# Three projection and post-processing steps moved by one place in the step table of one attention layer

## The chip, the cores and the metric

The kernel runs on one core of a Trainium2 chip. The metric is the device time of one launch in microseconds (us), the median of three executions. A profiled execution gives the trace from which all rows below come. The core has a matrix engine (PE, its weight loads are shown as PEld), a vector engine (DVE), a scalar engine (ACT), a general engine (POOL) and a queue engine (SP) that here only issues DMAs. POOL issues small DMAs too. The engines run on their own and meet at semaphores.

## What is computed

Four transformer blocks follow each other on x of 4 batches x 256 tokens x 256 channels, with one context of the same shape. The first has two cross-attentions with 16 heads of 128 channels and an MLP; the second one cross-attention with 16 heads of 16 channels and an MLP; the third is the one that the change touches; the fourth is a grouped-query attention and a layer norm. Cut to what matters, the third is:

```python
h = jnp.concatenate([x, latents], axis=1)          # 256 context rows, then 256 token rows: 512 keys
q = (latents @ q_w + q_b).reshape(b, k_len, 16, 16)
kv = (h @ kv_w + kv_b).reshape(b, p + k_len, 16, 16, 2)
attn = jnp.einsum('bkhd,bnhd->bhkn', q, kmat) / 16
attn = jnp.where(full_mask, attn, -jnp.inf)        # the mask covers the context keys
attn = jax.nn.softmax(attn, axis=-1)
attn_out = einsum('bhkn,bnhd->bkhd', attn, v) @ out_w + out_b + residual
out = rmsnorm(attn_out, postnorm_w)
out = jax.nn.gelu(out @ mlp_w1 + mlp_b1) @ mlp_w2 + mlp_b2
return out + residual
```

Here `x` is the context and `latents` are the 256 tokens that the block before left.

## The kernel before

One program is written out for all five engines by hand. Every operation stands in an engine's stream in the order in which Python emits it, and waits with `wait_ge` on semaphores that count what others have done. Numbers that PE multiplies are split into a high and a low part; a projection is three matmuls (lines 125 to 127: high by high, high by low, low by high) for each half of the channels.

The layers after the first block are made by the `heads_*` functions (lines 1934 to 2311), layer 2 being the one of the change. It works in steps. A step handles two units (a unit is 128 queries of one head against all 512 keys), so a batch of 16 heads is 16 steps (`TB`), four batches are 64 steps, and 7 more drain the pipeline. Below, "step n" is the n-th of these, and "place k" is n modulo 16 inside a block of 16. In step n

- PE multiplies queries by keys for the two units of step n (line 1983, 512 columns each, three PSUM banks in turn), then keys by queries for the two units of step n-5 (line 2001, four matmuls of 256 columns, two banks), then at places 1, 5, 9 and 13 the weighted sums of four heads (line 2069), then the table's post and preparation work of this step, then filler matmuls on constant tiles (line 2113) where the step has neither sums nor a projection: two, or one if the step has post work (`fill_step`). At even steps it ends with the transpose of the row maxima of the two steps before (line 2079).
- DVE takes the row maxima of the two units (line 2236): the first, then the table's work, then the second.
- ACT copies the transposed maxima to `rows` (line 2173), does its part of the table's work, then the exponentials of the two units of step n-5 (line 2159).
- POOL splits the maxima into two parts (lines 2274 and 2276), for the transpose, and sends the finished rows by two small DMAs into the query tile Q (line 2290), where the matmuls of line 2001 read them at the third step after the transpose.

What else is done when is set by two tables. `IN_LAYER[2]` prepares the next batch (b = 1, 2, 3, in blocks 0, 1, 2): `q0 q1` and `k0 k1` project queries and context keys on PE into one bank, `x0 x1` the token keys into another, `v0 v1` and `v2 v3` the values; `qh`, `kh`, `xh` are the high parts on ACT (line 1602, one step later), `ql`, `kl`, `xl` the low parts on DVE (line 1641, one step later); `maskrow` is made on POOL (line 1708, two steps later). `q_out`, `k_out`, `x_out` and `mask_out` are DMAs of SP that spread these parts over the partitions of the tiles Q and K of the next batch: six DMAs for each of q, k and x (line 1468) and two for the mask (line 1491). SP has no steps: it takes its list in order and waits at each entry for what that needs. `POSTS[2]` finishes the batch before, in blocks 1, 2 and 3 (table place k is step 16b+6+k, so 4 is place 10): `po0` and `po1` are four transposes each on PE of the summed heads (line 1738), `on0` and `on1` are a reciprocal and a product on DVE one step later (lines 1772 and 1774). `po1` uses the bank that `on0` reads, and waits for it:

```python
w.wait_ge(S["h_on"], s.po(b, q))                    # L1736
for g in range(4):
    z = pe.transpose(s.MB[:, g * 128:g * 128 + 128], ...)
```

At step 48, so behind the last of these DMAs, SP's list has four weight loads of 256 KB (`piece_sp`, line 277), which wait until the parts that stood in the same staging tile have been sent (`spread_done`). A batch's first step waits (`ready`, line 1964) until its Q and K are complete.

Of the kernel before, what the change touches and what calls it, by code (L numbers as in the profile page):

```python
# [1123 lines left out]
def attn_end(c, w):  # L1124
# [49 lines left out]

# [2 lines left out]
HELD = {1: ("kvtq", "tkqv"), 2: ("kvtqxw", "tqkvw"), 3: ("kvtq", "tqkv")}  # L1177

POSTS = {1: {2: ["po0", "on0"], 3: ["po1", "on1"], 4: ["onT", "oth"], 5: ["otl"], 6: ["c0"], 7: ["c1", "y"]},
# [3 lines left out]

# [1309 lines left out]
```

## Time and profile before

| | |
|---|---|
| Median of three executions | 1269.28 us (1266.02, 1269.28, 1271.29) |
| The profiled execution | 1269.28 us, of which the trace spans 1267.8 us |
| PE / PEld busy | 1223.9 us (97%) / 1033.9 us (82%) |
| DVE / ACT / POOL busy | 891.0 us (70%) / 783.1 us (62%) / 600.0 us (47%) |
| Mean granted PE clock | 0.994 of full speed |
| Layer 2's steps 0 to 63 | from 860.7 to about 1001 us |

Busy time is what the instructions take from start to end. Matmuls overlap, so a busy PE can still be one that waits a little at each instruction; the start of one instruction to the start of the next tells more than its duration. Rows of the timeline merge equal instructions that follow each other; in brackets stands how long the engine had been idle and what ended it. The granted clock is 1.0 at 2.4 GHz and 0.5 at 1.2 GHz.

### The profile page before, as it was taken

Reading aid. Unit: us, or ns where it says so; the run is one execution under the profiler, and the core shown is the slowest. Engines: PE = TensorE matmul, PEld = TensorE weight load, DVE = VectorE, ACT = ScalarE, POOL = GpSimd, SP = SyncE. Lnnn points to the kernel's source line nnn. Section 1 sums busy time; section 2 is a strip of 40 time slices with the busy share of each in tenths; the row PEclk is TensorE's granted clock in tenths of the full one; section 3 lists DMA queues with packets and bytes.
Section 4 is the critical chain, followed back from the end, with each engine's and each line's share of the span. In section 5 each row is a group of like instructions: output and inputs, shape, how many; then the busy total and the mean of one; then the engine's idle time right before and its main releaser. Section 6 shows DMA issues by size and latency. Waiting matters only on the chain. (4 is left out here: it accounts for less than half of the span.)

```text
span 1267.8 us, 27226 instructions
## 1 busy us (share of the span) xinstructions
PE 1223.9 (97%) x9982; PEld 1033.9 (82%) x9982; DVE 891.0 (70%) x2304; ACT 783.1 (62%) x1889; POOL 600.0 (47%) x966
## 2 busy tenths in 40 slices
PE   8999999999999999999989999899999889999997
PEld 7999999999999999999978565786665578666664
DVE  5887867779877777878855776536677664667764
ACT  4876666668866666667864655756665653555553
POOL 3884555558865554556841533504443331334333
PEclk9999999999999999999999999999998999999999
DMA  5441001104420100101411220122212012121100
GB/s 170 152 139 32 29 26 32 33 27 133 134 85 26 34 26 26 34 26 58 123 34 51 80 79 3 51 77 85 73 59 64 2 57 74 53 69 37 45 11 18
DMA packets 56820, 75.03 MB, mean 59 GB/s; under 512 B 11312, under 2 KB 30576, under 8 KB 56688
## 3 DMA queue, kind: packets, MB, share of 16 engines
q1 hardware_dynamic: 51568, 72.75, 18.7%
q8 instruction: 79, 1.29, 0.4%
q0 software_dynamic: 5120, 0.56, 0.3%
q14 instruction: 53, 0.43, 0.1%
HBM read 49.46 MB, written 1.05 MB: 40 GB/s over the span
## 5 line engine op out<-in xcount | busy, mean ns | idle before, releaser
L1095 POOL TENSOR_SCALAR E<-E,rl 128x256 f32<-128x256 f32 x256 | 243.6, 962 | 210.1 <-DVE rl L980 210.1
L2159 ACT ACTIVATE PT<-bank 128x512 f32<-128x512 f32 x320 | 176.5, 593 | 112.4 <-PE bank L2012 56.0
L846 ACT ACTIVATE QTh<-bank,bqs 128x256 fp32r<-128x256 f32 x128 | 60.8, 475 | 156.1 <-PE bank L127 155.9
L2242 DVE CUSTOM_DVE_ANT_0 Em<-bank,M 128x256 bf16<-128x256 f32 x256 | 95.1, 420 | 53.8 <-PE bank L1987 22.3
L856 ACT ACTIVATE E<-bank,nm 128x257 f32<-128x257 f32 x256 | 119.5, 481 | 1.2 <-DVE nm L950 1.1
L984 DVE TENSOR_TENSOR PTl<-bank,PTh 128x512 fp32r<-128x512 f32 x128 | 88.0, 687 | 27.3 <-ACT PTh L868 26.8
L2236 DVE TENSOR_REDUCE nm<-bank 128x1 f32<-128x512 f32 x128 | 83.6, 684 | 33.1 <-PE bank L1983 30.5
L2001 PE MATMUL bank<-Q,K 51*128 51x256 f32 (+1 forms) x640 | 104.1, 323 | 2.8 <-DMA Q<-rows 0.9
L957 DVE SCALAR_TENSOR_TENSOR QTl<-bank,bqs,QTh 128x256 fp32r<-128x256 f32 x128 | 61.5, 481 | 64.0 <-ACT KT L847 63.2
L868 ACT CAST PTh<-bank 128x512 fp32r<-128x512 f32 x128 | 75.2, 588 | 43.1 <-PE bank L771 43.1
L2290 POOL DMA_DIRECT2D Q<-rows x96 | 54.4, 568 | 95.5 <-ACT rows L2173 95.5
L950 DVE TENSOR_REDUCE nm<-bank 128x1 f32<-128x257 f32 x256 | 95.4, 414 | 3.4 <-PE bank L127 3.4
L2069 PE MATMUL bank<-PT,V 128*32 128x256 f32 x1280 | 87.4, 392 | 2.6 <-ACT PT L2159 2.6
L125 PE MATMUL bank<-KT,QTh 128*128 128x258 f32 x256 | 83.3, 326 | 3.4 <-issue 3.2
L2001 PEld LDWEIGHTS bank<-Q,K 51*128 51x128 f32 (+1 forms) x640 | 67.6, 187 | 20.4 <-ACT PT L2159 10.1
L771 PE MATMUL bank<-ident,E 128*128 128x128 f32 x512 | 76.7, 272 | 0.0
L990 DVE SCALAR_TENSOR_TENSOR OTl<-bank,cols,OTh 128x256 fp32r<-128x256 f32 x128 | 60.7, 474 | 18.2 <-ACT OTh L874 18.2
L126 PE MATMUL bank<-KT,QTh 128*128 128x258 f32 x256 | 73.3, 286 | 0.0
L2285 POOL DMA_DIRECT2D Q<-rows x64 | 37.7, 591 | 74.1 <-ACT rows L2173 71.2
L127 PE MATMUL bank<-KT,QTl 128*128 128x258 f32 x256 | 72.3, 282 | 0.0
L125 PE MATMUL bank<-PTh,Vh 128*128 128x256 f32 x256 | 71.8, 281 | 0.0
L127 PE MATMUL bank<-PTh,Vl 128*128 128x256 f32 x256 | 71.7, 280 | 0.0
(438 smaller groups left out, 4423.2 us busy)
## 6 DMA issues: line engine op xcount, KB each, us to landing
stage<-in_wts SPq DMA_DIRECT2D x99, 256.0 KB, 3.3
U<-in_vrows SPq DMA_DIRECT2D x64, 256.0 KB, 2.7
K<-stage SPq DMA_DIRECT2D x48, 128.0 KB
Q<-stage SPq DMA_DIRECT2D x48, 128.0 KB
K<-stage SPq DMA_DIRECT2D x48, 64.0 KB
Q<-stage SPq DMA_DIRECT2D x48, 64.0 KB
K<-xh SPq DMA_DIRECT2D x16, 128.0 KB, 2.9
Q<-rows POOLq DMA_DIRECT2D x96, 4.0 KB, 1.8
```

The source lines that it names most:

```text
L125: pe.matmul(o, wh, xh, start=first, stop=False, skip_group_check=skip)
L127: return pe.matmul(o, wl, xh, start=False, stop=last, skip_group_check=skip)
L771: m = pe.transpose(s.PTB[:, k * 256 + t * 128:k * 256 + t * 128 + 128], s.E[:, i % 3, t, k * 128:k * 128 + 128], c.ident[:])
L856: m = act.activation(s.E[:, i % 3, t, 0:257], bank[:, 0:257], ACT.Exp, bias=s.nm[:, r, t:t + 1], accum_out=s.ls[:, r, t:t + 1])
L950: dve.tensor_reduce(s.nm[:, r, t:t + 1], bank[:, 0:257], AX.X, ALU.max, negate=True).then_inc(S["dve_max"])
L984: dve.tensor_tensor(s.PTl[:], s.PTB[:].rearrange("p (a b) -> p a b", a=2), f32(s.PTh[:]), ALU.subtract).then_inc(S["dve_pt"])
L1095: m = pool.tensor_scalar(s.E[:, i % 3, t, 0:256], s.E[:, i % 3, t, 0:256], s.rl[:, r, t:t + 1], None, ALU.mult)
L2001: z = pe.matmul(s.STB[y][:, 256 * e:256 * e + 256], s.K[r][at, q // s.rp, o:o + 128], s.Q[r][at, q // s.blocks, :], start=l != 3 or e == 0 ...
L2069: z = pe.matmul(s.OB[32 * q:32 * q + 32, 0:256], s.V[b % s.NV][:, k, (4 * g + q) // s.rep, :], s.PT[(i0 + q) % s.NPT][:, k, :], start=k == ...
L2159: act.activation(s.PT[i % s.NPT][:, 2 * u:2 * u + 2, :].rearrange("p a b -> p (a b)"), s.STB[y][:], ACT.Exp).then_inc(S["t_ex"])
L2236: dve.tensor_reduce(nm[:, u:u + 1], bank[:], AX.X, ALU.max, negate=True).then_inc(S["t_mx"])
L2242: dve.tensor_tensor_reduce(out=s.Em[:, (2 * i + e) % 4], in0=bank[:, e * 256:e * 256 + 256], in1=s.M3[:, j, e, :], scale=-1.0, scalar=3.4e ...
```

## The change

Only the two tables change, and only for layer 2.

```diff
@@ IN_LAYER
             2: {0: ["mask", "v2-", "v3-", "vb-"], 2: ["turn", "th", "tl"], 3: ["res"],
-                4: ["q0", "q1", "qh", "ql", "maskrow"], 6: ["k0", "k1", "kh", "kl", "q_out"],
-                8: ["x0", "x1", "xh", "xl", "mask_out", "k_out"], 10: ["v0", "v1", "va", "x_out"]},
+                4: ["q0", "q1", "qh", "ql", "maskrow"], 6: ["k0", "k1", "kh", "kl"], 7: ["x0", "x1", "xh", "xl"],
+                8: ["mask_out", "q_out"], 9: ["k_out"], 10: ["v0", "v1", "va", "x_out"]},
@@ POSTS
-         2: {4: ["po0", "on0"], 6: ["po1", "on1"], 8: ["onT", "oth", "otl"], 13: ["c0", "c1", "y"]},
+         2: {5: ["po0", "on0"], 6: ["po1", "on1"], 8: ["onT", "oth", "otl"], 13: ["c0", "c1", "y"]},
```

The projection of the token keys goes from place 8 to place 7, with its parts on ACT and DVE. `fill_step` follows by its own rule: the filler pair leaves place 7 and comes to place 8. `po0` with `on0` goes from place 10 to place 11, where it stands one step ahead of `po1`; place 11 has then one filler instead of two. In SP's list the two mask DMAs stand ahead of the six of the queries.

On ACT, places 7 and 8 of block 0 (`xh` is the high part of the token keys, `PT` the exponentials, `rows` the maxima):

```order
 L2159 ACTIVATE PT_15138<-bank 128x512
 L2159 ACTIVATE PT_15139<-bank 128x512
-L2159 ACTIVATE PT_15138<-bank 128x512
-L2159 ACTIVATE PT_15139<-bank 128x512
-L2173 CAST rows_15145<-bank 8x128
 L1602 ACTIVATE xh_14373<-bank,cols_51 128x256 x2
+L2159 ACTIVATE PT_15138<-bank 128x512
+L2159 ACTIVATE PT_15139<-bank 128x512
+L2173 CAST rows_15145<-bank 8x128
```

The two instructions of `xh` now stand ahead of the exponentials of step 8 and of the row copy of step 9.

On DVE, places 10 to 13 of block 1 (`V` is the value tile, `rl` and `On` the reciprocal and the product of `on0`, then of `on1`; `nm` the maxima):

```order
 L1652 TENSOR_TENSOR V_14370<-bank,vb_14375 128x16x16 x2
+L2236 TENSOR_REDUCE nm_15143<-bank 128x1 x2
 L1772 RECIPROCAL rl_15148<-bank 128x16
 L1774 TENSOR_TENSOR On_15147<-bank,rl_15148 128x256
-L2236 TENSOR_REDUCE nm_15143<-bank 128x1 x4
+L2236 TENSOR_REDUCE nm_15143<-bank 128x1 x2
 L1772 RECIPROCAL rl_15148<-bank 128x16
 L1774 TENSOR_TENSOR On_15147<-bank,rl_15148 128x256
```

Two maxima, the second of step 11 and the first of step 12, now stand ahead of `on0`, and two instead of four lie between `on0` and `on1`.

In SP's list, block 2, with the semaphores that each entry waits for (`mrow` is the mask, `stage` holds the query parts and then the context key parts):

```order
 L1479 DMA mraw_14371<-in_mask 128x256
-L1468 DMA Q_15133<-stage_54 16x4x512 [waits s_hq,s_t_st]
+L1491 DMA K_15134<-mrow_14372 1x8x512 [waits s_t_st,s_mask_row]
+L1491 DMA K_15134<-mrow_14372 1x8x512
+L1468 DMA Q_15133<-stage_54 16x4x512 [waits s_hq]
 L1468 DMA Q_15133<-stage_54 16x4x512 x3
 L1468 DMA Q_15133<-stage_54 16x4x512 [waits s_lq]
 L1468 DMA Q_15133<-stage_54 16x4x512
-L1491 DMA K_15134<-mrow_14372 1x8x512 [waits s_mask_row]
-L1491 DMA K_15134<-mrow_14372 1x8x512
```

The first DMA of the chain waits for the mask row, and the query DMAs stand behind it.

## Rows read from the trace of the kernel before

**Rows 1.** The page's head and its first part, busy time by engine.

```profile
span 1267.8 us, 27226 instructions
...
PE 1223.9 (97%) x9982; PEld 1033.9 (82%) x9982; DVE 891.0 (70%) x2304; ACT 783.1 (62%) x1889; POOL 600.0 (47%) x966
```

**Rows 2.** Timeline, places 7 to 9 of block 1: start, duration, engine, line.

```profile
908.45 0.50 PE L1983 MATMUL bank<-K,Q 49*128 49x512 f32 x2
...
908.72 0.82 ACT L1602 ACTIVATE stage<-bank,cols 128x256 fp32r<-128x256 f32 x2
...
909.12 0.60 PE L2113 MATMUL bank<-units 128*128 128x512 bf16 x2
...
909.45 1.05 ACT L2159 ACTIVATE PT<-bank 128x512 f32<-128x512 f32 x2
...
909.65 0.58 PE L1983 MATMUL bank<-K,Q 49*128 49x512 f32 x2
...
910.98 0.39 PE L125 MATMUL bank<-hTh,W5x 128*128 128x256 f32 x1
...
912.71 0.50 PE L1983 MATMUL bank<-K,Q 49*128 49x512 f32 x2
```

**Rows 3.** Timeline, places 10 to 12 of block 1.

```profile
915.24 0.50 PE L1983 MATMUL bank<-K,Q 49*128 49x512 f32 x2
...
918.05 0.50 PE L1983 MATMUL bank<-K,Q 49*128 49x512 f32 x2
...
919.19 0.74 DVE L1652 TENSOR_TENSOR V<-bank,vb 128x256 f32<-128x256 f32 x2
919.25 0.57 PE L1983 MATMUL bank<-K,Q 49*128 49x512 f32 x2
...
919.85 0.25 DVE L1772 RECIPROCAL rl<-bank 128x16 f32<-128x16 f32 x1
920.13 0.42 DVE L1774 TENSOR_TENSOR On<-bank,rl 128x256 f32<-128x256 f32 x1
...
920.47 1.88 DVE L2236 TENSOR_REDUCE nm<-bank 128x1 f32<-128x512 f32 x3
920.61 0.66 PE L1738 MATMUL bank<-ident,OS 128*128 128x128 f32 x4 [0.16 <-DVE On L1774]
921.10 0.38 PE L2113 MATMUL bank<-units 128*128 128x512 bf16 x1
...
921.74 0.27 PE L2079 MATMUL bank<-ident,np 128*8 128x128 f32 x1 [0.26 <-POOL np L2276]
```

**Rows 4.** Windows, places 13 to 15 of blocks 1 and 2: stretch, length, busy, clock, DMA.

```profile
921.95:927.35 5.40, 5.40 (x59) 3.18 (x58) 4.33 (x9) 3.82 (x10) 2.10 (x6) 1.00 0.01 1
957.39:966.71 9.32, 8.43 (x60) 4.43 (x59) 4.25 (x9) 3.90 (x9) 2.05 (x5) 0.63 0.17 62
```

**Rows 5.** The chain that ended last, piece by piece, at step 45.

```profile
954.71 4.04 DMA Q<-rows
```

**Rows 6.** Timeline of SP, POOL and PE: the DMA chains of blocks 0 and 2.

```profile
884.11 1.26 SPq L1468 DMA_DIRECT2D K<-xl  x2
...
892.59 0.49 PE L1983 MATMUL bank<-K,Q 49*128 49x512 f32 x2
...
940.13 3.77 SPq L1468 DMA_DIRECT2D Q<-stage  x6
...
942.57 1.08 POOL L1708 TENSOR_SCALAR mrow<-mraw 128x256 fp32r<-128x256 int32 x1
...
954.02 1.92 SPq L277 DMA_DIRECT2D stage<-in_wts  x4
```

**Rows 7.** DMA issues from 860 to 1000 us, size, median from issue to landing.

```profile
stage<-in_wts SPq DMA_DIRECT2D x4, 256.0 KB, 4.1
Q<-rows POOLq DMA_DIRECT2D x61, 2.0 KB, 2.0
K<-xl SPq DMA_DIRECT2D x6, 128.0 KB, 2.9
```

## The prediction

> **What bounds the kernel now.** I read the page's busy times first: PE is busy for 1223.9 of a 1267.8 us span, DVE for 891.0 [rows 1]. So a step costs what PE does in it, unless PE stands. Then I laid the timeline over layer 2, step by step, by the starts of line 1983 with which PE opens each step. The steps are regular: a step without extra work is 1.20 us, one with a projection near 2.4, one with the weighted sums 2.53. Three kinds of wait stand out, and the change touches all three.
>
> Places 7 and 8 [rows 2]. Place 7 is short: 908.45 to 909.65, of which queries and keys are 0.67 (to the fillers at 909.12) and the filler pair 0.53. ACT has the high part of the keys in it (908.72) and ends its exponentials only at 909.45 + 1.05 = 910.50, 0.85 us into place 8. The keys there need the bank, so the projection starts at 910.98, 1.33 after the step's start where 0.67 would do: 0.66 us lost.
>
> Places 10 to 12 [rows 3]. Place 10 is 2.81 us (915.24 to 918.05), place 11 1.20, place 12 2.70 (919.25 to 921.95, where the windows named below begin). In place 12 PE waits 0.16 for the product `on0` and 0.26 for the maxima, which DVE does late since it has the values and `on0` in place 11.
>
> Places 13 to 15 of block 2 [rows 4]. The windows give 9.32 us where the same steps of block 1 take 5.40. The chain of waits shows a `Q<-rows` DMA of 4.04 us [rows 5], ending at 958.75, for which PE stood (9.32 less the busy 8.43 is 0.89 us); and the granted clock of the stretch is 0.63 against 1.00. So 3.92 us are lost in this one place: 0.89 to the wait, about 3.0 to matmuls at the 1.2 GHz level. The clock fell behind a place 12 like the one above, with its two waits, and this wait after it. Why are the rows late? SP issues four weight loads of 256 KB from 954.02 on [rows 6], and the rows are issued beside them. Over the layer such rows land 2.0 us after issue, the weights 4.1 [rows 7].
>
> **The change, part by part.** Sums are made against the profiled execution, 1269.28 us, which is also the median of the three runs; about 1.5 us of it lie outside the span and stay.
>
> *Projection to place 7, three times (blocks 0 to 2).* Nothing is removed: 12 matmuls of the projection change places with two fillers. Before, places 7 to 9 take 912.71 - 908.45 + 2.53 = 6.79 us (the last is a step of weighted sums, 915.24 - 912.71 [rows 2, 3]). After, place 7 is 0.67 + (912.71 - 910.98 - 0.21) = 2.19: the 0.21 is the transpose of the maxima, which only even steps have (921.74 to 921.95 [rows 3, 4]). In 2.19 us ACT is through at 2.05 (908.45 to 910.50), so the keys of place 8 don't wait. Place 8 is 0.67 + 0.53 + 0.21 = 1.41, and now ACT has `xh` in it, the same two instructions as `kh`: it ends near 2.05 after the step's start, 0.64 into place 9, against 0.85 before. The lost 0.66 becomes at most 0.45 and moves to place 9; as place 8 has no row copy on ACT ahead of `xh`, I take 0.35. Sum 2.19 + 1.41 + 2.53 + 0.35 = 6.48, so -0.3 each and -0.9 for three. Bounds: 0 (the wait moves whole) and -0.66 each, -2.0 in all (it goes whole). DVE isn't late: two maxima and `xl` are under 2 us a step, and place 9 has 2.5. `x0` waits for no bank that place 7 still uses, since token keys have a bank of their own for b > 0.
>
> *`po0` and `on0` to place 11, three times (blocks 1 to 3).* Place 10 loses four transposes, which stand 0.49 ahead of what follows them (920.61 to 921.10): 2.81 - 0.49 = 2.32. Place 11 becomes 0.67 + 0.49 + one filler. Two fillers were 0.53, so one is about 0.25: 1.41. Then place 12. On DVE, counted from the start of place 11 (918.05), the values start at 1.14 and what follows them at 1.80. Before, that was `on0`, and the maxima came at 2.42. Now two maxima come first, at 0.60 each (three in 1.88 with the last one's 0.69): the reciprocal starts at 3.00, the product 0.28 later at 3.28, and PE's `po1`, which started 0.48 after the product did (920.13 to 920.61), can start at 3.76. In PE's own order it could start at 1.41 + 0.67 = 2.08. So PE stands about 1.7 us less what its keys wait for ACT anyway (0.69 in the row now: 919.25 to 920.61 less 0.67). Behind `po1` in PE's stream are one filler, the transpose of the maxima and all of step 13; POOL's rows and ACT's exponentials wait for them in turn. From 3.76 it is 0.49 + 0.25 + 0.21, so place 12 ends at 4.71. The transpose doesn't wait any more, its maxima are ready by 2.49 + 0.6. Places 10 to 12: 2.32 + 4.71 = 7.03 against 6.71 before, +0.3 each, +0.9 for three. (Block 3 has a transpose of the next norm instead of the values at place 10; I take the same.) Bounds: if DVE gets at `on0` a maximum earlier, by 0.6, the places get 0.3 shorter than before each (-0.9 in all); if the first maximum of place 12 starts later because its queries do, I add 0.3 each (+1.8).
>
> The two edits cancel: 0, between -2.9 and +1.8.
>
> *SP's list.* A chain is issued without a break: 940.13 to 954.02 is 13.89 us for 20 DMAs [rows 6]. It now starts when the mask row is there, 942.57 + 1.08 = 943.65, and not at 940.13. So it ends 3.5 us later: 957.5 for the weights. If an issue now and then waits less, 956.8. Two things hang on it. First, the token keys must have landed before the batch's first step. Block 0 is the tightest: the last issue ends at 884.11 + 1.26 = 885.37, lands 2.9 after its start [rows 6, 7], by 888; 3.5 later is under 892 and step 16 starts at 892.59. Cost 0, with about 1 us in hand, and more in blocks 1 and 2. Second, the weight loads no longer meet the rows that PE waits for at step 45; those have only key DMAs beside them and land after about 2.0, in time. The next pair follows places 11 and 12 later, at 954.71 + 3.90 = 958.6 by the times before, amid the weights. With 4.04 us it lands at 962.65. It is needed in step 47, 0.33 after its start: 957.39 + 5.40 - 1.20 + 0.33 = 961.9 [rows 4, 5]. (The shift of these places by 0.3 moves both.) So the wait is between 0 and 0.75 us; I take 0.5, near the row of the same kind (0.89) and less, as the weights are then under way and not just starting.
>
> The row shows that a pair of 2 KB DMAs takes twice as long beside weight loads (4.04 against 2.0). The Trainium skill, "DMA: Bandwidth & Descriptors", section on queues, rings and completion order, says that each DMA engine goes round its queues in turn, packet by packet; by that rule alone a small DMA on another queue would hardly be held up and this wait would be 0. The trace doesn't agree with it here, and I go by the row.
>
> *The clock.* It is the largest term, 3.0 us, and the one that no row settles. What the rows show is that it fell once in layer 2's steps of block 2, after a place 12 and a wait of 0.89 us. In block 1, without that wait, the same places ran at 1.00 [rows 4]. After the change the wait behind step 44 is gone, but places 11 and 12 take 4.7 us for hardly more matmuls than they did in 3.9, in three blocks: PE stands for over 1 us in one piece. I think the clock falls in one of the three, for a price between 1.5 (half of what it cost) and 3.0; value 2.5. So of the 3.92 lost now, 2.5 + 0.5 = 3.0 are lost then: -0.9. Bounds: -3.9 (nothing lost) and +5.6 (three falls at 3.0 and the wait at 0.5, less the 3.92).
>
> Sum: 1269.28 - 0.9 + 0.9 - 0.9 = 1268.4 us.
>
> **Rivals.**
> 1. *All clear.* The rows come in time and the clock stays: 1269.28 - 3.9 + 0 = 1265.4. For it: the collision of rows 5 is moved away by 3.5 us. Against: the weights still need 4 us somewhere, and place 12 gets thinner.
> 2. *The thin place 12 drops the clock in each block.* `po1` waits over 1 us for `on0`, PE's work in places 11 and 12 gets too thin, and the following weighted sums run at 1.2 GHz three times: +5.6, with edit two at +0.3 a block more (+0.9): 1275.8, slower than before. It decides from a place 12 of about 3.3 us on, that is if `on0` is as late as worked out. For it: the clock fell at just this place in block 2. Against: in block 1 it stood at 1.00. Beside it, the Trainium skill, "TensorE: Matmul & The Clock Gate", section on the second failure mode of the clock gate, tells of a kernel whose clock swung because PE idled briefly between groups of matmuls; by that page this rival would be the rule; in rows 4 it happened in one block of two.
> 3. *Late token keys.* If the later chain is stretched by 0.1 us an issue, block 0's keys land 2 us later than worked out and step 16 waits 1 us; blocks 1 and 2 don't. 1268.4 + 1.0, and a fall of the clock behind it, 1271.9.
> 4. *Nothing of it shows.* The wait only moves from step 45 to 47 with its fall of the clock, and the edits cancel: 1269.3. It lies inside the forecast's own range.
>
> **How the numbers follow.** The forecast, with rival 4, has 0.62 at 1268.4; all clear 0.19; rival 2 0.12; rival 3 0.05; the rest 0.02. Three runs of the same kernel lie 5.3 us apart, so a change under 0.5% (6.3 us, 1262.9 to 1275.6) can't be told from none. All clear reaches beyond -0.5% only with the lower bound of both edits (1265.4 - 2.9): 0.04. Rival 2 is at the upper edge, and half of it is beyond: 0.08 with what the others add. Same: 0.88. The range goes from 1263.5 (all clear, with half its bound) to 1275 (short of rival 2's full price).
>
> **What would show it.** Places 7, 8, 9 at 2.2, 1.4 and 2.7 to 3.0 us, with ACT's `xh` ahead of the exponentials. Place 11 at 1.4 and place 12 near 3.3, with PE idle for about 1 us before line 1738, ended by the product. The four weight loads near 957, and no wait for `Q<-rows` at step 45; if there is one, at step 47. The granted clock by block tells which rival holds: below 1.00 in none, one or three of the blocks 1 to 3. I would be wrong if place 12 doesn't get longer, if step 16 waits for DMAs of K, or if anything outside layer 2 moves by more than the clock does.

## The result, and the profile after

The changed kernel takes 1273.96 us (median of 10 runs, 1271.58 to 1278.85), the kernel before beside it 1268.1 (10 runs, 1265.46 to 1271.29). The ratio is 1.0056, 95% interval 1.0041 to 1.0072: 5.9 us slower by the medians, 7.1 by the ratio, where the forecast said 0.9 faster. The profiled execution of the changed kernel took 1277.74 us, span 1276.3, against 1269.28; PE's busy time answers to [rows 1].

```profile
span 1276.3 us, 27220 instructions
...
PE 1226.1 (96%) x9979; PEld 1035.4 (81%) x9979; DVE 890.4 (70%) x2304; ACT 782.2 (61%) x1889; POOL 598.9 (47%) x966
```

PE is 2.2 us busier, and the span is 8.5 us longer: 6.3 us of the difference between these two profiles is PE standing, not work (both have stretches at the lower clock). I laid the steps of both traces side by side by the starts of line 1983. Places 7 to 9 and 10 to 12 came out much as worked out. Here are places 8, 9 and 10 of block 1 in the changed kernel, to be held against [rows 2, 3] (columns: start, duration, engine, line):

```profile
909.65 0.50 PE L1983 MATMUL bank<-K,Q 49*128 49x512 f32 x2
...
911.92 0.50 PE L1983 MATMUL bank<-K,Q 49*128 49x512 f32 x2
...
913.24 0.54 PE L1983 MATMUL bank<-K,Q 49*128 49x512 f32 x2
...
916.19 0.50 PE L1983 MATMUL bank<-K,Q 49*128 49x512 f32 x2
```

The steps are 2.27, 1.32 and 2.95 us, 6.54 in all where there were 6.79. The loss begins in place 12 and becomes large in place 13. The same block, places 11 to 13:

```profile
918.59 0.50 PE L1983 MATMUL bank<-K,Q 49*128 49x512 f32 x2
...
918.67 3.20 SPq L1468 DMA_DIRECT2D K<-xh  x4
...
919.25 1.12 POOL L2290 DMA_DIRECT2D Q<-rows  x2 [2.92 <-ACT rows L2173]
...
920.06 0.50 PE L1983 MATMUL bank<-K,Q 49*128 49x512 f32 x2
...
920.40 1.28 DVE L2236 TENSOR_REDUCE nm<-bank 128x1 f32<-128x512 f32 x2
...
921.87 0.42 DVE L1774 TENSOR_TENSOR On<-bank,rl 128x256 f32<-128x256 f32 x1
...
922.35 0.65 PE L1738 MATMUL bank<-ident,OS 128*128 128x128 f32 x4 [1.35 <-DVE On L1774]
...
923.26 0.50 PE L1983 MATMUL bank<-K,Q 49*128 49x512 f32 x2
...
926.00 0.80 PE L2001 MATMUL bank<-Q,K 51*128 51x256 f32 x4 [2.23 <-DMA Q<-rows]
926.72 3.64 PE L2069 MATMUL bank<-PT,V 128*32 128x256 f32 x32
930.29 0.79 PE L1983 MATMUL bank<-K,Q 49*128 49x512 f32 x2
```

Two waits stand one behind the other: 1.35 us for `on0` (DVE has two maxima ahead of it, as worked out), and then 2.23 us for the rows that POOL issued in place 11. The weighted sums behind them (line 2069) take 3.64 us for what is 1.93 at full clock. So the step of place 13 is 7.03 us where it was 2.53. The chain of waits has the DMA itself, and the same in block 2, to be held against the 4.04 of [rows 5]:

```profile
919.80 6.15 DMA Q<-rows
...
965.29 5.37 DMA Q<-rows
```

The windows show what the engines and the DMA did there (columns: length, PE, PEld, DVE, ACT, POOL busy, then clock, DMA share, GB/s): SP's chain of loads in block 1, places 13 to 15 of block 1, places 13 to 15 of block 2, answering to [rows 4].

```profile
917.40:925.40 8.00, 5.01 (x36) 3.30 (x34) 5.98 (x14) 3.33 (x8) 2.60 (x6) 0.98 1.15 159
...
923.26:933.78 10.52, 8.29 (x60) 4.32 (x59) 3.87 (x8) 3.93 (x9) 2.08 (x6) 0.68 0.38 52
964.08:971.67 7.59, 5.58 (x59) 3.09 (x58) 5.05 (x9) 3.83 (x9) 2.97 (x8) 1.00 0.66 175
```

Places 13 to 15 of block 1 cost 10.52 us instead of 5.40; those of block 2 7.59 instead of 9.32, with the wait moved from step 45 to 47 (2.02 us) and the clock lower just behind it. The DMA share is 1.15 in the first row (it adds up the time of packets, so it can pass 1) and yet only 159 GB/s are moved. SP's loads in the kernel before, over the corresponding stretch, read

```profile
914.70:920.70 6.00, 5.76 (x50) 3.92 (x43) 3.99 (x10) 3.18 (x8) 1.49 (x4) 1.00 0.68 198
```

that is, 198 GB/s at 0.68. This pair of rows turned out to be the key to block 1. Where the 8.5 us of the two profiles are, by starts of line 1983: 1.4 ahead of layer 2, blocks 0 to 3 of it -0.1, +5.2, -1.5 and +5.0, and -1.5 behind it. Block 3 has neither SP's key loads nor a new wait but the 1.27 us for `on0`; nearly all of its 5.0 is clock (steps of weighted sums of 4.1 us for 2.5). One profile says little on the clock, as it differs from run to run; but each run has its mean granted clock. Over 108 runs of six kernels (before, changed, e1 to e4), fitted with one level per kernel and one common slope, each 0.001 of that mean goes with 1.00 us, and the rest scatters by about 1 us. The mean clock is 0.996 before (35 runs) and 0.991 for the changed kernel (25 runs): some 5 us by the clock, and 2.9 us at equal clock. (These 25 runs of the changed kernel have a mean 8.0 us above that of the 35 before, which is the sum of the two parts.)

DMA issues of the layer, size and median from issue to landing, against [rows 7]:

```profile
K<-xh SPq DMA_DIRECT2D x12, 128.0 KB, 3.5
stage<-in_wts SPq DMA_DIRECT2D x4, 256.0 KB, 5.3
Q<-rows POOLq DMA_DIRECT2D x58, 2.0 KB, 2.0
```

The rows' median hasn't moved: what hurts are single pairs, and a median hides them.

### The profile page after: what moved, and what is told of

Same layout as the page of the kernel before. It is cut to its first block and busy times, and to the rows that moved or that the text cites. A ratio compares the mean times of both kernels' runs of the same rounds, so it can differ in the third digit from the quotient of the medians.

```text
span 1276.3 us, 27220 instructions
## 1 busy us (share of the span) xinstructions
PE 1226.1 (96%) x9979; PEld 1035.4 (81%) x9979; DVE 890.4 (70%) x2304; ACT 782.2 (61%) x1889; POOL 598.9 (47%) x966
```

## The experiments

Every kernel ran beside the kernel before. "Clock" is the mean granted clock over a kernel's runs; the kernel before beside it had 0.996 for e1 to e4, e8, e9, e11, e12, e16 and e17, and 0.995 for e5 to e7, e10, e13 to e15 and e18. "Step 29" is the length of place 13 of block 1 in the kernel's profile, in us. All kernels have 11 or 12 runs but the changed one in its first comparison (10) and e13 (8).

| kernel | median us | ratio | 95% interval | clock | step 29 |
|---|---|---|---|---|---|
| changed | 1273.96 | 1.0056 | 1.0041-1.0072 | 0.991 | 7.03 |
| e1_list | 1271.19 | 1.0032 | 1.0019-1.0045 | 0.993 | 3.55 |
| e2_x7 | 1267.81 | 1.0004 | 0.9991-1.0017 | 0.995 | 2.53 |
| e3_po | 1270.58 | 1.0022 | 1.0006-1.0038 | 0.994 | 2.53 |
| e4_x7_po | 1268.46 | 1.0013 | 1.0001-1.0025 | 0.994 | 2.53 |
| e5_list_x7 | 1272.29 | 1.0031 | 1.0016-1.0045 | 0.993 | 5.99 |
| e6_list_po | 1274.46 | 1.0041 | 1.0027-1.0055 | 0.992 | 2.78 |
| e7_after_spread | 1272.10 | 1.0030 | 1.0018-1.0041 | 0.992 | 6.02 |
| e10_after_paced | 1271.29 | 1.0021 | 1.0011-1.0030 | 0.994 | 4.22 |
| e8_x7_spread | 1265.65 | 0.9987 | 0.9974-1.0000 | 0.996 | 2.53 |
| e9_spread | 1265.77 | 0.9989 | 0.9977-1.0001 | 0.996 | 2.53 |
| e11_po_fill | 1267.66 | 0.9998 | 0.9986-1.0011 | 0.996 | 2.53 |
| e12_po_first | 1267.97 | 1.0001 | 0.9989-1.0013 | 0.995 | 2.53 |
| e13_after_fill | 1273.22 | 1.0047 | 1.0030-1.0064 | 0.994 | 6.13 |
| e14_list_spread | 1266.37 | 0.9987 | 0.9976-0.9998 | 0.996 | 2.53 |
| e15_x7_spread_first | 1265.20 | 0.9976 | 0.9962-0.9989 | 0.996 | 2.53 |
| e16_list_x7_spread | 1272.39 | 1.0033 | 1.0019-1.0046 | 0.993 | 6.07 |
| e17_after_mended | 1264.37 | 0.9980 | 0.9967-0.9992 | 0.996 | 2.53 |
| e18_gap_spread | 1269.99 | 1.0007 | 0.9992-1.0023 | 0.994 | 3.26 |

**One edit at a time.** e1 has the list, e2 the projection, e3 `po0`/`on0`, e4 the last two together. The lines are those of the tables, against the kernel before:

```diff
 e1  -  6: [.. "kh", "kl", "q_out"], 8: ["x0", "x1", "xh", "xl", "mask_out", "k_out"]
     +  6: [.. "kh", "kl"], 8: ["x0", "x1", "xh", "xl", "mask_out", "q_out"], 9: ["k_out"]
 e2  +  7: ["x0", "x1", "xh", "xl"], 8: ["mask_out", "k_out"]
 e3  +  2: {5: ["po0", "on0"], ...
```

> Only the order of the loads on SP is changed: q_out stands behind mask_out (place 8), k_out at place 9; the projection stays at place 8 and po0/on0 at place 10. Theory L (the later, uninterrupted chain of SP meets the rows pair and PE stands for it): the rows needed at place 13 of block 1 come over 4 us after issue, PE stands about 2 us at step 29 and the clock falls there; block 2's wait moves from step 45 to 47. The kernel is about +5 us, 1273. Rival P (the thin place 12 drops the clock): places 10 to 12 are as in the kernel before, so the wait of block 2 goes away and nothing comes in its place: 1265 to 1268. Rival B (both are needed together): 1268.

> Only the projection x0, x1, xh, xl goes from place 8 to place 7; the loads on SP keep their order, po0/on0 stay at place 10. Theory L and rivals P and B all say the same: places 7 to 9 get 0.24 us shorter in each of three blocks (6.79 to 6.55), block 1 runs at full clock, the wait at step 45 stays: 1268.1 - 0.7 = 1267.4. If the shift alone moved the rows into the loads, it would be over 1270.

> Only po0 and on0 go from place 10 to place 11. Theory L: places 10 to 12 get 0.36 us longer in each of three blocks, PE waits 1.3 us for on0 in place 12, the clock does not fall more often than before: 1268.1 + 1.1 = 1269.2. Rival P: the longer wait in place 12 drops the clock in block 1 and in block 3 at full price, 3 us each: 1273 or more. Rival B: 1269.2.

> The whole change but for the order of the loads on SP: projection at place 7, po0/on0 at place 11, q_out at place 6 ahead of mask_out. Theory L: 1268.1 - 0.7 + 1.1 = 1268.5, no wait for rows at step 29. Rival P: as the changed kernel, 1273 to 1274. Rival B (both needed together): 1268.5.

Measured: the list costs 0.32% (4 us), `po0`/`on0` 0.22% (2.8 us), the projection nothing that can be told from 0; e4 came where the sum had it (1268.5). Theory L and rival P were each half right: the list loses, but 4 us and not 5, and `po0`/`on0` loses more than 1.1 us, but less than 5. At equal clock, by the fit above, the list costs 1.7 us, `po0`/`on0` 0.8 and the projection -0.5; the rest of each is clock. e1's profile has the wait in both blocks, but small in block 1 (0.75 us, places 13 to 15 then take 6.44) and full in block 2, where the weight loads are (2.25 us):

```profile
922.80:929.24 6.44, 5.69 (x59) 3.18 (x59) 4.34 (x9) 3.82 (x10) 2.10 (x6) 1.00 0.20 58
959.33:967.73 8.40, 6.15 (x59) 3.15 (x58) 5.46 (x10) 4.26 (x10) 2.99 (x8) 0.92 0.61 159
```

**Two edits, and the weight loads taken away.** e5 is the changed kernel with `po0`/`on0` back, e6 with the projection back. e7 and, later, e8, e9 and e14 to e18 spread the four weight loads over the last block. e10 paces the token keys' loads as well.

```diff
 e7, in heads_sp, at n == 3 * s.TB
-            for k in PIECES_AT[2].values():
+            for i, k in enumerate(PIECES_AT[2].values()):
+                g = 24 + i
+                w.wait_ge(S[f"dma_rows{g % 2}"], 32 * ((s.o["g"] + g) // 2 + 1))
                 piece_sp(c, k)
 e10, beside that, in heads_prep_sp, x == "x_out"
+        if b > 0:
+            g = 8 * b - 4
+            w.wait_ge(S[f"dma_rows{g % 2}"], 32 * ((s.o["g"] + g) // 2 + 1))
```

> The changed kernel with po0/on0 back at place 10: SP's new list and the projection at place 7. Over all runs so far each 0.001 of the mean granted clock went with 1.00 us, and by that the list alone cost 1.7 us at full clock and 1.8 by the clock, po0/on0 alone 0.8 and 2.0, the projection alone -0.5 and +1.2. If the edits only add up, this kernel is at the list's time less nothing: 1271 (+3.5 against before). If the list needs the 0.4 us that the projection brings forward in order to meet the rows of block 1 fully, it is at 1273 with a wait over 1.5 us at step 29.

> The changed kernel with the projection back at place 8: SP's new list and po0/on0 at place 11. If the edits only add up, 1267.7 + 3.5 + 2.9 = 1274. If the fault needs all three, it is below 1272. In the trace the step of place 13 in block 1 has the wait for the rows (1.0 us in the kernel with the list alone).

> The changed kernel, but SP issues the four weight loads of 256 KB one by one in the last block, each when the rows of steps 51, 53, 55 and 57 have landed, not in a row behind the token keys of the last batch. If the meeting of rows and weight loads is the main part of the loss, the waits at steps 45 and 47 go (2.0 us in the changed kernel) with their fall of the clock (about 1.5): 3 us faster than the changed kernel, 1271. If block 1 holds the loss (rows beside K's own loads, where no weights are), it stays at 1273 to 1274.

> As the kernel before it in this list (weight loads spread over the last block), and SP issues the token-key loads of the next batch only when the rows that POOL issues in place 11 have landed. Theory L: both meetings of rows with big loads are taken away, the wait at step 29 shrinks from 2.2 us to under 0.5, and the time comes down to that of the kernel with the old list (1268.5). Rival P (the thin place 12 alone lowers the clock): 1271 or more, with the clock falling behind place 12 though no rows are late. Rival Q (the loads of the keys' high and low parts, which are already under way when the rows are issued, hold them up, not the token keys behind them): the wait at step 29 stays over 1 us.

Measured: e5 has the full meeting in its profile (1.62 us of wait at step 29), but its median, 1272.3, lies between the two expectations, and by the ratio it is no slower than the list alone (1.0031 for 1.0032): in its profile it has lost the wait of e1 at step 47 (0.25 us for 2.25). e6 is 1274.5 as the sum said. Spreading the weights takes 1.9 us off the changed kernel by the medians (1.0056 to 1.0030), between the two expectations; the wait at step 47 goes, but block 1 keeps one of 1.61 us, and in block 2, where no rows are late now, the clock fell all the same (7.10 us for places 13 to 15, at 0.76). Pacing the token keys shortens the landing of the pair from 4.1 and 5.5 us to 2.8 and 3.3, and no wait for rows is left at step 29. Yet the time is 1271.3 and not 1268.5: what rival P foretold, and the clock did fall in place 13 of that profile (4.22 us) behind the 1.35 us for `on0` alone. Beside that, in block 0 the held-back keys are late:

```profile
894.37 0.50 PE L2006 MATMUL bank<-Q,K 51*128 51x256 f32 x4 [0.96 <-DMA Q<-rows]
896.36 0.50 PE L1988 MATMUL bank<-K,Q 49*128 49x512 f32 x2 [0.96 <-DMA K<-xl]
```

The second row is step 16 waiting for its token keys: rival 3 of the prediction, brought about by issuing them 2.5 us later than the change does (3.3 us after place 11 began, for 0.8). By these rows the remedy loses in block 0 (0.96 twice) what it saves at step 29 (1.61), so its time can't decide between theory L and rival P.

**The two waits by themselves.** e8 and e9 spread the weights under the old list. e11 puts four fillers into PE's wait for `on0`; e12 shortens that wait by taking `on0` ahead of the first maxima on DVE (the call behind them is left out where it has been made).

```diff
 e11, in heads_pe, ahead of the posts
+        if l == 2 and "po1" in steps:
+            w.wait_ge(S["m_x"], 4 * l)
+            w.wait_ge(S["t_os"], s.o["os"] + s.attended_by(n - 1))
+            w.wait_ge(S["t_rows"], s.o["g"] + s.turned_by(n - 1))
+            ones(s.OB, 4)
 e12, in heads_dve, ahead of the step's first maxima
+        b, steps = s.posts_at(n - 1)
+        if l == 2 and "on0" in steps:
+            for x in steps:
+                heads_post_dve(c, s, b, x)
```

> Projection at place 7, old order of SP's list, po0/on0 at place 10, and the four weight loads issued one by one in the last block, each when the rows of steps 51, 53, 55 and 57 have landed. If the weight loads are what meets the rows at step 43 in the kernel before (wait 0.89 us, fall of the clock 3 us), both go: 1268.1 less the projection's 0.3 and 2 to 3 = 1265. If the fall of the clock in block 2 comes without that wait as well, 1267.5.

> The kernel before with only the weight loads spread over the last block. If the meeting at step 43 costs what the profile of the kernel before shows (0.89 + 3.0, though not in each run), 1265.5; if only the wait goes, 1267.2; if the loads hurt as much in the last block, 1268 or more.

> po0/on0 at place 11 as in the kernel with that edit alone (1270.6, +2.9), and four filler matmuls (about 1.0 us) in PE's stream ahead of po1, where PE stands 1.35 us for on0. Theory: the clock falls because PE stands there; busy with fillers it falls no more often than before, and 0.8 us (full clock) stays: 1268.9, mean clock near 0.996. Rival: the clock part of po0/on0 has nothing to do with that wait: 1270.6 and a mean clock near 0.994, or slower by the fillers.

> po0/on0 at place 11, and DVE takes on0 ahead of the first maxima of place 12, not behind it: PE's wait for on0 gets 0.6 us shorter (1.35 to about 0.7). Theory: places 10 to 12 are no longer than in the kernel before and the clock recovers in part: 1268.5. Rival: DVE's maxima get late instead, and the time stays at 1270.6.

Measured: spreading the weights alone gives 0.9989 (0.9977 to 1.0001, so it may be nothing), and the meeting of [rows 5] was worth about 1.4 us in a mean run, not the 3.92 of that one profile. Block 2 then reads like block 1:

```profile
958.00:963.40 5.40, 5.40 (x59) 3.19 (x59) 4.33 (x9) 3.82 (x10) 2.09 (x6) 1.00 0.02 4
```

The fillers are the cleanest single test of the clock here. They add four matmuls in each of three blocks and take the loss of `po0`/`on0` from 1.0022 to 0.9998, a difference of 0.24%, of which noise could make about 0.20 (an estimate from the two intervals). Place 12 of block 1 in e3, and then in e11:

```profile
923.24 0.66 PE L1738 MATMUL bank<-ident,OS 128*128 128x128 f32 x4 [1.36 <-DVE On L1774]
```

```profile
920.93 1.04 PE L2113 MATMUL bank<-units 128*128 128x512 bf16 x4
922.36 0.66 PE L1738 MATMUL bank<-ident,OS 128*128 128x128 f32 x4 [0.39 <-DVE On L1774]
```

The step is 3.20 us in both: the work behind `on0` comes no sooner, and what is gained (the clock from 0.994 to 0.996, over 12 runs each) is gained because PE doesn't stand. It is the mean that shows this and no single profile: in e3's own the clock is 1.00 in places 13 to 15 of blocks 1 and 2 in spite of the waits. e12 does it the other way: a wait of 0.76, a step of 2.60 us instead of 3.20, and the loss is gone too (1.0001). Its clock stays at 0.9945, hardly above e3's 0.9941, so its gain is in the shorter steps.

**What is left.** e13 is the changed kernel with e11's fillers; e14 the list alone with the weights spread; e15 the candidate: old list, projection at place 7, weights spread, `po0`/`on0` at place 11 with e12's order on DVE.

> The changed kernel with four filler matmuls ahead of po1 in place 12, where PE stands 1.35 us for on0. With po0/on0 alone the same fillers took 2.5 us off the loss. If the edits add up here too: 5.9 - 2.9 + 0.4 = 3.4, so 1271.3. If the wait for the rows of block 1 lowers the clock by itself there, the fillers give less: 1273 or more.

> SP's new list with the weight loads spread over the last block; the projection at place 8, po0/on0 at place 10. The list alone is +3.5. Without the weights the wait at step 47 (2.25 us, with its fall of the clock) goes. If that was the list's main cost: 1266 to 1267, near the kernel before with its loads spread (1265.8). If K's own loads beside the rows of block 1 are the main cost: 1269 or more.

> The old list, projection at place 7, weight loads spread over the last block, po0/on0 at place 11 with on0 ahead of DVE's first maxima. Projection and spread loads together are -1.6; on0 first takes the 2.9 of po0/on0 down to 0.3. So 1267.7 - 1.6 + 0.3 = 1266.4; it beats x7_spread only if places 10 to 12, which are 0.2 us shorter each than in the kernel before in that trace, show at full clock: 1265.0.

Measured: in the changed kernel the fillers give no more than can be told from 0 (1.0056 to 1.0047, intervals overlap), as a wait of 1.72 us for rows stays behind them at step 29; the 1271.3 expected of adding up was wrong, and the rival right. e14 decides for the weights: once none stand behind the list it costs nothing (0.9987 against 0.9989 for e9). e15 is faster than the kernel before, 0.9976 (0.9962 to 0.9989), by 3 us; from e8 and e9 its interval can't tell it.

**The pair that makes block 1.** e16 is e14 with the projection at place 7. e17 is the changed kernel with all three remedies: e7's, e10's for block 1 alone (`if b == 2`), e12's.

> New list and projection at place 7, weight loads spread over the last block, po0/on0 at place 10. The same with the projection at place 8 was 1266.4. Theory: the list alone has the token keys' loads start 0.4 us later against the rows of block 1 (they wait for xh), the projection at place 7 has them run on from the keys' loads without a gap, so PE waits about 1.6 us at step 29 with a fall of the clock: 1268.5 to 1269.5. Rival: the wait is po0/on0's doing, whose row of places is what shifts the rows: 1266.

> The changed kernel with all remedies: weight loads spread, the token keys' loads of block 1 issued when the rows of step 27 have landed, on0 ahead of DVE's first maxima in place 12. The theory (three meetings: weights and rows, token keys and rows, PE and on0) says the loss of 5.9 us goes, and it stands at about the kernel before with its loads spread, 1266 to 1267. If it stays above 1269, a part of the cause is not named.

Measured: two edits that each cost nothing without the weights (e8 0.9987, e14 0.9987) give 1.0033 together (e16), 0.44% above e9. Place 13 of block 1 has this wait:

```profile
925.26 0.51 PE L2003 MATMUL bank<-Q,K 51*128 51x256 f32 x4 [1.66 <-DMA Q<-rows]
```

The theory had foretold the sign but too little (1268.5 to 1269.5 for 1272.4). And e17 takes the whole loss away: 0.9980, where the kernel before with its loads spread (e9) has 0.9989. So no part of the loss outlasts the three remedies; the pacing was not run with the old list, so how much it gives by itself isn't known. (Block 1 of e17 still has one wait of 1.30 us for a maximum, behind the paced loads, that I didn't follow up.)

What differs between e14 and e16 is not the list's pace, 0.65 us an issue in both. Nor is it what the expectation of e16 said, a list that holds the token keys' loads back: in both their first issue follows the last of the context keys by 0.65 us. It is the DMA engines. SP's key loads of block 1 in each:

```profile
917.30:921.30 4.00, 4.00 (x38) 3.01 (x31) 2.03 (x4) 1.84 (x5) 0.61 (x3) 1.00 0.73 203
```

```profile
917.80:920.80 3.00, 3.00 (x24) 2.19 (x22) 1.56 (x4) 1.56 (x4) 0.92 (x2) 1.00 1.15 163
```

203 GB/s at a share of 0.73 in e14, 163 at 1.15 in e16. In the trace's packets of SP's queue that is 52 ns each on average against 105 ns. SP issues 128 KB every 0.65 us, which is 200 GB/s. In the quick condition the engines keep up with that at a share of about 0.7; in the slow one they move less than is issued. So there a backlog builds up (the four `K<-xh` of block 1 land 4.7, 5.0, 5.2 and 5.7 us after issue in the changed kernel, the first two 3.0 and 3.35 in e1), and POOL's 2 KB rows, issued in the same stretch, are late with them.

The slow condition begins before the token keys, in the loads of the context keys. The first four us of these in block 1, in the changed kernel and in e1:

```profile
914.76:918.67 3.91, 3.91 (x49) 2.73 (x41) 2.32 (x4) 2.11 (x5) 0.98 (x4) 1.00 0.91 183
```

```profile
914.44:918.34 3.90, 3.90 (x51) 2.84 (x44) 3.02 (x6) 2.63 (x6) 1.28 (x4) 1.00 0.68 203
```

All profiles, one per kernel, sort the same way. The nine kernels with the old list have it in no block. With the new list, no gap and the projection at place 7 block 1 is slow in all seven (changed, e5, e7, e10, e13, e16, e17; packets of 84 ns or more in the median of this stretch), and with the projection at place 8 in none of three (e1, e6, e14; 46 or 47 ns). So the projection's place goes with it, though it moves nothing in SP's list; one profile per kernel doesn't say how. In e17 the context keys' loads are slow too, and yet no wait for rows comes, since the token keys' loads are held back behind the rows.

The kernel before has the mask's two small DMAs between the last query load and the first context key load, which are issued 2.1 us apart instead of 0.65; for 1.3 to 1.4 us of this the engines move 19 to 30 GB/s. With the new list the key loads run on without a gap. e18 tests this: e7 with a gap again in blocks 1 and 2, 3.1 us from issue to issue in block 1, 2.0 of it with no traffic at all.

```diff
 e18, in heads_prep_sp, x == "k_out"
+        if l == 2 and b >= 2:
+            w.wait_ge(S["dma_hq"], 64 * s.spreads(b + 1))
+            w.wait_ge(S["dma_lq"], 32 * s.spreads(b + 1))
```

> The changed kernel with the weight loads spread (1272.1, +3.8 against before), and SP issues the keys' loads of the last two batches (in blocks 1 and 2) only when the query loads ahead of them have landed. Theory: the slow stretch of the DMA engines in block 1 (155 GB/s at a busy share of 1.15 where the kernel before has 200 at 0.7) comes from the keys' loads running into the query loads' tail; with the gap it is gone, the rows of step 27 land within 3 us, PE waits less than 0.3 at step 29, and the time is 1268 to 1269. Rival: the slow stretch comes with K's loads wherever they stand, then the wait at step 29 stays, since the loads only come later: 1272 or more.

Measured: 1270.0 (1.0007, 0.9992 to 1.0023) against e7's 1272.1 (1.0030, 1.0018 to 1.0041), where 1268 to 1269 was expected; the intervals just overlap. The key loads of block 1 are quick again:

```profile
921.00:927.00 6.00, 4.65 (x27) 2.76 (x28) 3.99 (x10) 2.49 (x6) 2.05 (x6) 0.73 0.65 182
```

The pair of step 27 lands in 2.4 and 3.9 us instead of 4.1 and 5.5, and PE doesn't wait for it. In block 0 of the same run, which has no gap, the slow condition now appeared (about 100 ns a packet) and PE waited 1.2 us at step 13; e6 has the same in its block 0, with 1.50. So the slow condition is gone in the two blocks that have the gap. Not each chain without a gap is slow, though: e1, e6 and e14 have none in block 1, the changed kernel none in block 0, and these ran quick. What tips one into it is open.

## Why the prediction was wrong

The step that failed is the one on SP's list, in the sentence that the pair of step 43 and its like "have only key DMAs beside them and land after about 2.0, in time". I had taken the weight loads for what holds up the rows, since [rows 5, 6] show them there, and the rows' median of 2.0 us [rows 7] for all others. But beside 128 KB key loads they can be later still: 4.46 and 6.15 us in block 1, where the prediction had no wait at all and PE stood 2.23 us. Even in block 2 the pair of step 43 itself took 3.0 and 3.3, just in time. The prediction asked of the later chain whether the token keys land in time for the next batch (they did, cost 0) and whether weights meet rows in block 2; it didn't ask which loads now stand beside the rows of block 1. The second step that failed is the gain set against it: the sum took off 3.92 us that one profile showed at step 45 and put back 3.0 for the clock and step 47. In a mean run about 1.4 were there to be taken off (see 4).

1. *Projection to place 7.* Right: 6.54 for 6.79 us in each block (-0.25; forecast -0.3), places at 2.27, 1.32, 2.95. In whole runs it is 1.0004, a gain too small to show. What it does beside the new list (e16 against e14) the prediction had nowhere.
2. *`po0`/`on0` to place 11.* Right in its rows: place 11 1.46 us, place 12 3.20 (forecast 3.3), +0.36 a block (forecast +0.3), the wait 1.35 (forecast 1.7 at most). What came behind it was mis-sized, see 4.
3. *SP's list.* The chain came 4.1 us later against place 11 (block 2), not 3.5, as the mask row itself was done 0.6 us later against it; the token keys were in time for step 16, as worked out. The wait at step 45 went and one at step 47 came, as forecast, but 2.02 us for 0.5 (bounds 0 and 0.75): the pair took 5.37 us and not 4.04. That weights "under way" are milder than weights just starting was the wrong way round. In the six profiles of the old list with the weights in a row the pair's second DMA was issued 0.1 to 0.7 us after the first weight load and took 3.2 to 4.4 us; in the five of the new list, 0.9 to 1.7 us after it, it took 5.4 to 5.8, beside quick key loads (e1, e6) as beside slower ones. And block 1 was missed. By rows the waits for `Q<-rows` are 4.5 us in the layer where they were 0.9.
4. *The clock.* I set one fall in three blocks at 2.5 us, against a loss of 3.92 that is taken off. The 3.92 was one profile's; removing its cause (e9) is worth about 1.4 in the mean. And rival 2, which got 0.12, is in kind what e3 and e11 show: a PE that stands 1.35 us ahead of `po1` in each block costs 2 us by the clock, and fillers there bring it back. Its full price, 5.6 us, was too much: in the profiles of e3 and e11 places 13 to 15 of blocks 1 and 2 ran at 1.00. Of the changed kernel's whole loss some 5 us are clock and 2.9 are not, where the forecast had a small gain in both together.

On the rule of the Trainium skill that I had weighed ("DMA: Bandwidth & Descriptors", queues, rings and completion order: an engine goes round its queues packet by packet): the runs again don't bear out what I made of it, that a small DMA on another queue is hardly held up; a 2 KB DMA of the rows took 1.6 us at its quickest and 6.15 beside the key loads.

The rule that would have helped is the one named with rival 2, from the Trainium skill, "TensorE: Matmul & The Clock Gate", second failure mode, brief idling of PE between groups of matmuls; e11 agrees with it (clock 0.994 to 0.996 by fillers in a wait alone).

## What to carry to other kernels

When a chain of loads is moved, look at each small transfer that runs beside any part of it, in every repetition, and take the worst landing of such a pair rather than the median; and ask whether the move closes a gap between two trains of loads: here the closed gap went with loads that moved more slowly than they were issued. The three waits of 1.35 us on PE (e3) were paid twice, 0.8 us by themselves and 2 by the clock, and fillers in the wait paid for themselves. Edits that cost nothing one by one can cost something together, so test them in pairs. A loss seen in one profile isn't the loss of a mean run: compare the mean clock over all runs before a fall of the clock is entered as a gain to be had.

## What the runs showed of the hardware

- The same loads at the same pace moved at two rates: packets of 52 ns, 203 GB/s, share 0.73 (e14); or of 105 ns, 163 GB/s, share 1.15 (e16; 159 in the changed kernel). The slow condition was in no block of the nine profiles with 2.1 us or more between the issues of the last query load and the first key load, in block 1 of all seven with the new list and the projection at place 7, and gone where a gap was put back (e18).
- A 2 KB DMA issued 0.1 to 0.7 us after the first of four 256 KB loads landed in 3.2 to 4.4 us (six profiles), one issued 0.9 to 1.7 us after it in 5.4 to 5.8 us (five profiles).
- Two edits without cost (e8 and e14, 0.9987 each) came to 1.0033 together (e16).
- Each 0.001 of the mean granted clock went with 1.00 us of this kernel, over 108 runs, and the 35 runs of the kernel before among them range from 1264.4 to 1271.0 us, about three quarters of their variance by it.
- Twelve extra matmuls in three waits (e11) made a kernel 2.9 us faster by the medians (1.0022 to 0.9998).
